# Transposes and division of an attention context moved from TensorE to VectorE, GpSimd and ScalarE

## The reference

```python
x = L0_attn_hidden_states
xn = _layernorm(x, axis=-1)
s = _L0_attn_ref(xn, L0_attn_Wq, L0_attn_Wk, L0_attn_Wv, L0_attn_Wo)
g = _silu(_L0_ffn_ref(xn, L0_ffn_w_gate, L0_ffn_w_up, L0_ffn_w_down))
x = x + s * g
...
```

```python
q = (x @ Wq).reshape(b, t, N_HEADS, HEAD_DIM).transpose(0, 2, 1, 3)
k = (x @ Wk).reshape(b, t, N_KV, HEAD_DIM).transpose(0, 2, 1, 3)
v = (x @ Wv).reshape(b, t, N_KV, HEAD_DIM).transpose(0, 2, 1, 3)
q = _apply_rope(q, cos, sin)
k = _apply_rope(k, cos, sin)
k_h = jnp.repeat(k, GROUP_SIZE, axis=1)
v_h = jnp.repeat(v, GROUP_SIZE, axis=1)
scores = jnp.einsum('bhqd,bhkd->bhqk', q, k_h) / math.sqrt(HEAD_DIM)
causal = jnp.triu(jnp.ones((t, t), dtype=bool), k=1)
scores = jnp.where(causal[None, None], jnp.finfo(scores.dtype).min, scores)
attn = jax.nn.softmax(scores, axis=-1)
ctx = jnp.einsum('bhqk,bhkd->bhqd', attn, v_h)
ctx = ctx.transpose(0, 2, 1, 3).reshape(b, t, D_OUT)
return ctx @ Wo
```

## Time and profile before

| | |
|---|---|
| three executions | 1332.64, 1336.5, 1327.77 us, median 1332.64 |
| the profiled execution | 1332.45 us, its span 1330.7 us |
| mean granted clock of TensorE | 0.98 of full speed |
| busy share of the span | PE 91%, PEld 68%, DVE 61%, ACT 49%, POOL 29% |
| the chain that ended last, by engine | PE 71%, DVE 14%, ACT 8%, issue 4%, DMA 2% |
| instructions | PE 8860, DVE 1322, ACT 1106, POOL 460 |

### The profile page before, as it was taken

One profiled execution on the slowest core, in us unless ns is written; L12 is line 12 of the kernel. 1 busy time (PEld: TensorE's weight loads), 2 busy tenths in 40 slices (PEclk: granted clock), 3 DMA queues, 4 the chain that ended last, 5 costly groups with the idle time before them and its releaser, 6 DMA issues.

```text
span 1330.7 us, 22702 instructions
## 1 busy us (share of the span) xinstructions
PE 1216.5 (91%) x8860; PEld 900.0 (68%) x8860; DVE 808.3 (61%) x1322; ACT 652.6 (49%) x1106; POOL 385.9 (29%) x460
## 2 busy tenths in 40 slices
PE   4999999999999999979999999999899889898897
PEld 3788876666656556546777787776666666676664
DVE  8743467665675645674655566536776776765444
ACT  3333357555454555554333333336665655565653
POOL 1000125333210101021344434405532342424443
PEclk9999989999999999979999999899999999999999
DMA  6000000110000100001242222120001001000001
GB/s 254 0 1 0 1 34 3 48 58 2 1 2 2 36 1 1 26 25 48 72 142 95 95 72 80 64 80 3 2 2 40 2 2 34 1 25 23 2 1 63
DMA packets 15259, 48.07 MB, mean 36 GB/s; under 512 B 2858, under 2 KB 6959, under 8 KB 14388
## 3 DMA queue, kind: packets, MB, share of 16 engines
q1 hardware_dynamic: 15156, 46.63, 10.1%
HBM read 44.00 MB, written 2.10 MB: 35 GB/s over the span
## 4 chain that ended last, share of the span: by engine, by line
PE 71%; DVE 14%; ACT 8%; issue 4%; DMA 2%; POOL 0%; POOLq 0%; DVEq 0%; ACTq 0%; SPq 0%
PE bank L650 18%; PE bank L766 14%; PE bank L680 8%; PE bank L909 8%; PE bank L869 6%; PE bank L817 4%; PE bank L783 3%; DVE negmax L1816 3%; ACT probs L1381 3%; PE bank L849 2%; ACT pv L1389 2%; PE bank L880 2%; DMA W_lo_whole<-in_w 2%; PE bank L797 1%; PE bank L826 1%
## 5 line engine op out<-in xcount | busy, mean ns | idle before, releaser
L1816 DVE TENSOR_REDUCE negmax<-bank 128x4 f32<-128x1024 f32 (+1 forms) x256 | 250.3, 1017 | 77.0 <-PE bank L826 66.2
L1381 ACT ACTIVATE probs<-bank 128x1024 f32<-128x1024 f32 (+1 forms) x256 | 218.0, 865 | 46.0 <-PE bank L849 37.7
L2023 POOL TENSOR_SCALAR_AFFINE_SELECT probs<-probs 128x512 f32<-128x512 f32 x192 | 125.9, 666 | 292.3 <-ACT probs L1381 292.1
L1966 POOL TENSOR_TENSOR W_lo<-W_lo_whole,W_hi 128x1536 fp32r<-128x1536 f32 x28 | 98.4, 3516 | 155.8 <-ACT W_hi L1132 155.8
L817 PE MATMUL bank<-kT,qT 64*128 64x256 f32 (+1 forms) x1024 | 110.5, 312 | 30.1 <-DVE negmaxT L1834 8.8
L817 PEld LDWEIGHTS bank<-kT,qT 64*128 64x128 f32 x1024 | 81.4, 191 | 65.9 <-issue 33.2
L869 PE MATMUL bank<-probs,V 128*32 128x256 f32 (+1 forms) x2048 | 119.6, 352 | 6.6 <-DVE negmax L1816 5.1
L1389 ACT ACTIVATE pv<-bank 128x256 f32<-128x256 f32 x128 | 49.2, 384 | 154.1 <-PE bank L869 153.6
L849 PE MATMUL bank<-qT,kT 64*128 64x256 f32 (+1 forms) x640 | 113.4, 384 | 3.7 <-DVE h_lo_whole L1638 1.6
L1132 ACT ACTIVATE W_hi<-W_lo_whole 128x1536 fp32r<-128x1536 f32 x28 | 41.7, 1488 | 130.6 <-DVE W_lo_whole L1592 130.6
L650 PE MATMUL bank<-xT_hi,W_hi 128*128 128x512 f32 x224 | 91.7, 410 | 5.6 <-ACT silu L1145 4.5
(11 more groups left out here) (205 smaller groups left out, 2692.3 us busy)
## 6 DMA issues: line engine op xcount, KB each, us to landing
W_lo_whole<-in_w SPq DMA_DIRECT2D x28, 768.0 KB, 4.1
Wqkv_lo_whole<-in_Wqkv SPq DMA_DIRECT2D x6, 768.0 KB, 6.7
Wo_lo_whole<-in_Wo SPq DMA_DIRECT2D x4, 1024.0 KB, 4.9
Wqkv<-in_Wqkv SPq DMA_DIRECT2D x2, 1536.0 KB, 7.5
...
```

The lines of the kernel that those rows point to most:

```text
L1381: nc.scalar.activation(A[l].probs[gi % 2][kb][:, :, q0 - kb * A[l].probs1:].rearrange("p (b h) q -> p b h q", b=2), B.tensor(key)[:, :, 0: ...
L1816: v.tensor_reduce(A[l].negmax[u % 2][:, qb, :].rearrange("p (b h) -> p b h", b=2)[:, :, 2 * g:2 * g + 2], B.tensor(key)[:, :, 0:2 * nk].re ...
L1966: gp.tensor_tensor(lo, whole, hi.bitcast(F32), ALU.subtract).then_inc(w_low.sem, 1)
L2023: gp.affine_select(out=blk, in_=blk, compare_op=ALU.is_ge, fill=0.0, base=0, pattern=[[0, 4], [1, P]], channel_multiplier=-1).then_inc(cau ...
```

## The change

The context is no longer turned by TensorE. After `take_pv`, VectorE's `turn_values` transposes `pv` (128x256, in SBUF) in blocks of 32x32 within the tile, which puts each head's sums in a column, and takes their reciprocals (128x8). GpSimd's `scale_context` multiplies the turned block by them (128x8x16), for two groups into one tile `scaled`. VectorE's `turn_context` turns that tile of a pair of groups in blocks of 32 again, in even slots, into one of RING = 6 context tiles of 128x256, whose rows stand as `project_out` needs them. In the layers with split products ScalarE's `context_high` rounds each such tile off and GpSimd's `context_low` takes the difference. `turn_rows`, `take_rows` and VectorE's `context_low` are gone, and so is the bank of turned contexts; `values_bank` is now 6, and 4 near the end of a run. The rows of the output weights are laid out in the new order by the host. `residual` uses the tile of the gate in place of `ctxr`. The split of the last output weights goes by the table `WO3_SLOTS`. In `ffn3` the last projection of outputs stands one chunk later. SP's loads are written as slots, as the other engines' are. In the diff below each engine's edits stand in this order: TensorE, ScalarE, VectorE, GpSimd.

```diff
+RING = 6
+WO3_SLOTS = {(10, 1): (0,), (10, 2): (1, 2), (10, 3): (3,)}
-def values_bank(l, U, g):
-
-    return 7 if not GQA[l] and g % 2 == 0 and U + 1 + g // 2 < RUN else 4
+def values_bank(U, g):
+
+    return 6 if U + 2 + g % 2 < RUN else 4
+def pair_turned(G):
+
+
+    return (G - 4) // 2 if G >= 4 and G % 2 == 0 else None
...
-            def turn_context(r, G, slot, bank=None):
...
-            def turn_rows(l, b, tau, bank):
...
-                pe.wait_ge(*B.emptied(("ctxT", l, b, tau)))
+                pe.wait_ge(*(ctx_low if GQA[l] else ctx_turned).at(l, 4 * (b + 1)))
...
-                if G >= 2:
-                    turn_context(r, G - 2, G)
...
-                for n in rows_turned(r, U, g):
-                    turn_rows(*n, OUT_BANK[n[2]])
...
-                        turn_context(1, last - 1, last)
                         weigh_values(1, last, last)
-                    if e == CHUNKS3_EARLY + 1:
-                        turn_context(1, last, last)
-                        for tau in range(2):
-                            turn_rows(3, SEQS - 1, tau, 6 + tau)
-                    if e == CHUNKS3_EARLY + 2:
+                    if e == CHUNKS3_EARLY + 3:
...
                 act.wait_ge(*B.filled(key))
+                if G >= 2:
+                    act.wait_ge(*values_turned.at(*next_of(r, G - 2)))
                 nc.scalar.activation(A[l].pv[gi % 2][:], B.tensor(key)[:, 0:SEQ], copy).then_inc(B.empties(key), 1)
...
-            def take_rows(l, b, tau):
...
+            def context_high(r, q):
+                l, qi = pair(r, q)
+                if GQA[l]:
+                    act.wait_ge(*ctx_turned.at(l, qi + 1))
+                    nc.scalar.activation(ctx_hi[r][:, q % RING, :], ctx_whole[r][:, q % RING, :], copy).then_inc(ctx_high.sem, 1)
...
                 if G >= 1:
                     take_pv(r, G - 1)
+                if pair_turned(G) is not None:
+                    context_high(r, pair_turned(G))
...
-                context(0, last - 1)
-                context(0, last)
+                turn_values(0, last - 1)
+                turn_context(0, last // 2 - 1)
+                turn_values(0, last)
                 scale_weights(CHUNKS2_EARLY + 1)
                 hidden(2, CHUNKS2_EARLY)
+                turn_context(0, last // 2)
...
-            def context(r, G):
+            def turn_values(r, G):
+
                 l, gi = group(r, G)
...
+                dve.wait_ge(*B.emptied(("PV", l, gi)))
                 if G >= 2:
...
+                    dve.wait_ge(*ctx_scaled.at(*next_of(r, G - 2)))
+                v.transpose(A[l].pvT[gi % 2][:].rearrange("p b r -> p (b r)"), A[l].pv[gi % 2][:]).then_inc(values_turned.sem, 1)
+                dve.wait_ge(*values_turned.at(l, gi + 1))
+                v.reciprocal(A[l].recip[gi % 2][:], A[l].pvT[gi % 2][:, :, HD]).then_inc(rs_ready.sem, 1)
+
+            def turn_context(r, q):
+
+                l, qi = pair(r, q)
+                if q >= RING:
+                    ll, qq = pair(r, q - RING)
+                    dve.wait_ge(*B.filled(("O", ll, qq // 4, 1)))
+                dve.wait_ge(*ctx_scaled.at(l, 2 * qi + 2))
+                v.transpose(ctx_whole[r][:, q % RING, :], A[l].scaled[q % 2][:].rearrange("p b r -> p (b r)")).then_inc(ctx_turned.sem, 1)
...
                 if G >= 2:
-                    context(r, G - 2)
+                    turn_values(r, G - 2)
+                if pair_turned(G) is not None:
+                    turn_context(r, pair_turned(G))
...
+            def scale_context(r, G):
+                l, gi = group(r, G)
+                q = G // 2
+                if q >= 2:
+                    ll, qq = pair(r, q - 2)
+                    pool.wait_ge(*ctx_turned.at(ll, qq + 1))
+                pool.wait_ge(*rs_ready.at(l, gi + 1))
+                gp.tensor_tensor(A[l].scaled[q % 2][:, :, HD * (G % 2):HD * (G % 2 + 1)], A[l].pvT[gi % 2][:, :, 0:HD],
+                                 A[l].recip[gi % 2][:].unsqueeze(2).to_broadcast([P, SEQ // 32, HD]),
+                                 ALU.mult).then_inc(ctx_scaled.sem, 1)
+
+            def context_low(r, q):
+                l, qi = pair(r, q)
+                if GQA[l]:
+                    pool.wait_ge(*ctx_high.at(l, qi + 1))
+                    gp.tensor_tensor(ctx_lo[r][:, q % RING, :], ctx_whole[r][:, q % RING, :],
+                                     ctx_hi[r][:, q % RING, :].bitcast(F32), ALU.subtract).then_inc(ctx_low.sem, 1)
...
                 if CAUSAL[l]:
                     cut_future(r, G)
+                if G >= 2:
+                    scale_context(r, G - 2)
...
+                if pair_turned(G) is not None:
+                    context_low(r, pair_turned(G))
```

More of the change, by code:

```diff
@@ L1765, in ffn3 @@
                     if e == CHUNKS3_EARLY:
[L1766 removed]
+                        turn_values(1, last)
+                        turn_context(1, last // 2 - 1)
                     if e == CHUNKS3_EARLY + 1:
[L1768 to L1771 removed]
+                        turn_context(1, last // 2)
+                    if e == CHUNKS3_EARLY + 3:
                         for tau in range(2):
@@ L2037, in slot @@
                     wqkv_low_part(3, g)
-                if r == 1 and U == 10:
-                    wo_low_part(3, g)
+                if r == 1:
+                    for c in WO3_SLOTS.get((U, g), ()):
+                        wo_low_part(3, c)
                 if r == 1 and (U, g) in SPLIT3_SLOTS:
```

209 lines of the change are left out of this document (95 added, 114 removed).

## The result

The changed kernel took 1300.95 us in the median of four executions (1296.24 to 1305.54). The ratio to the kernel before on the same chip is 0.9765, 95% interval 0.9737 to 0.9793. Measured again later beside other kernels it took 1296.94 us, ratio 0.9734 (0.9708 to 0.9761). I use 0.975 as the mean of the two, some 33 us of gain. The forecast was a gain of 16.6. The profiled execution is the slowest of its four, with a span of 1303.8 us.

The account below looks back on a forecast made before the run. TensorE was taken as the bound on average, gated in places by ScalarE's exponentials and VectorE's maxima. Terms -8.4, -9.1, +3.7 and -2.6 summed to -16.4 us, from 1332.45 to 1316 us; range 1280 to 1348.

Parts of the forecast that it names:

- What leaves TensorE: TensorE's removed matmuls: 128 pairs at 0.31 us and 32 fours at 0.49, a ceiling of 55.4 us.
- Layers 0, 2, 3: Attention slots of the split layers: 0.6 us gained per eight slots, 12 eights, with the last units -8.4 us in sum.
- Layer 1: Its 32 slots, without ScalarE's copy: 24 gain 0.31 us, 6 fours 0.49, two late slots cost 0.6 each; -9.1 us.
- Start of layer 2's feed-forward: Last output projection of layer 1 waits for VectorE's turn behind `hidden`: +2.0 us, +1.7 for the lower clock, +3.7.
- Start of layer 3's feed-forward: Two pairs, two fours and two waits go, 3.5 us, less 0.9 for the new chain over three engines: -2.6 us.
- TensorE bound in every slot: Rival for all slots: ScalarE is early, so all 55.4 us of removed TensorE work arrive, 1277 us; chance 0.16.
- VectorE as the new bound: Rival for first slots of 16 units: VectorE's turn takes 0.69 us, +12, so 1328 us, no change; chance 0.20.
- Exponentials held in all pairs: Rival for 48 slot pairs of split layers: ScalarE's exponentials wait 1.1 us for VectorE's turn, 1351 us; chance 0.14.
- GpSimd holding VectorE: Rival for VectorE's rotations and maxima's followers: GpSimd's 104 us of new work delays VectorE, +8, 1324 us; chance 0.10.

Follow-up runs that it names:

- the kernel with the early turn: The change with VectorE's last turn of layer 1 ahead of the feed-forward's hidden(2, 2) instead of behind it: 1292.4 us, ratio 0.9684 to the kernel before.

## Why the prediction was wrong in size

The direction, the durations and the main waits held, and the times lie in the stated range of 1280 to 1348. But the forecast of 1316 was short by half of the gain, for these steps.

**What leaves TensorE.** A pair was put at 0.31 us and costs 0.21 to 0.23 when put back, a four at 0.49 and costs some 0.43. The ceiling was thus some 42 us and not 55. This made the forecast too large, not too small.

**Layers 0, 2, 3: the step that failed.** I had -0.6 us for eight slots, 12 times. The table above has -2.0 to -2.5, so some -26 us for -7.2. Term by term: slot 1 of even units was to lose 0.7 and loses 0.53 to 0.84. Slot 2 was to gain 0.5 and does. The first of odd units was to gain 0.5, and gains 0.5 to 0.9. Slot 3 was to gain 0.8 and gains only 0.3 to 0.6, an error the other way. The other three slots of odd units were +0.1, -0.1, -0.1 and are -0.07, -0.28, -0.18. And slot 0 of even units gains 0.5 to 0.7, where I had listed nothing. The terms that I wrote down add up to -1.2; I then "made" 0.6 of them, so that this slot stood at a loss of 0.6 without a row. It was the largest single error, 1.2 us an eight, 14 us in all. What the slot gains is in part TensorE's stream and bank: the pair put back costs it 0.23 us, the old bank 0.1 to 0.2, and all together 0.4 of its 0.6; the other 0.2 stays open. The second are the other slots of odd units, -0.5 where I had -0.1, 5 us in all. In slots 1 and 3 I charged ScalarE's copy with 0.45 us, and it costs 0.13 and 0.04 (the run with the copy late); slot 2 has no copy, and there the old bank costs 0.2 to 0.4.

**Not costed at all: the bank.** The text went through every operation and never through `values_bank`. It is worth 6 to 10 us in time and 12.7 in undisturbed slots. It was in the view: L817 waits for `pv` 26 times before, 7.4 us. Part of it lies in the slots of the step above, so the two do not add.

**Layer 1**, forecast -9.1, has -9.8 in undisturbed slots (-8.3 in the second execution). In the profiled execution only -4.9 arrived with 34 us at the lower clock, in that of the second measurement -11.4 with 7; before had 20.

**Start of layer 2's feed-forward.** Forecast +3.7 with a wait of 3.7 us and a stretch at the lower clock. After:

```profile
622.41 3.54 DVE L1598 TENSOR_TENSOR h_lo<-h_lo_whole,h_hi 128x512 fp32r<-128x512 f32 x1 [1.47 <-ACT h_hi L1141]
625.87 0.43 DVE L1832 STREAM_TRANSPOSE ctxT_lo_whole<-scaled 128x256 f32<-128x256 f32 x1
...
626.45 1.19 PE L906 MATMUL bank<-Wo_lo_whole,ctxT_lo_whole 128*128 128x512 f32 x1 [2.63 <-DVE ctxT_lo_whole L1832]
```

The turn stands behind h_lo as said, 2.63 us, and the lower clock ran from 626.05 to 629.46. From the last weighing of run 0 to the first of run 1 the change lost 2.8 us in one execution (10 us at the lower clock, 7 before) and 0.7 in the other (7), less than the 3.7 forecast. **Start of layer 3's feed-forward**: forecast -2.6, but the stretch from the last weighing but one to the end took 65.1 us before and 66.8 and 66.1 after, both with 14 to 16 us of lower clock at the end where before had 1.5. That the clock hid the gain shows in the kernel with the early turn, whose code is the same here: it had 3.1 us of lower clock at the end and took 62.1, which is 3.0 less than before.

**The rivals.** TensorE bound in every slot would have given 1277. In undisturbed slots it is close (pairs at full price in most slots), in the time it is not. VectorE as the new bound fell, as its turn takes 0.43 us. Exponentials held in all pairs fell: ScalarE waited 4.5 us in 48 copies, all of it in eight of them. GpSimd holding VectorE is there but small: the rotation's four operations went from 97.7 us before to 106.7, 9 us more on VectorE, and fell to 99.1 without GpSimd's product; doubling the product cost some 3 us in undisturbed slots and nothing in the time.

**What stays open.** With TensorE's stream and bank as before, 11 us of gain are left. Undisturbed slots give +6 there, slot 1 of even units above all. In the first slots of odd units 1.1 us each went (8.24 to 7.15 in units 5 and 7 of run 1), and in slot 3 of unit 14 of run 0 4.6, where TensorE had waited 3.0 us for ScalarE's row copy, and where before had 3.4 us of lower clock. How the 11 us divide between such waits and the clock I can't say; the price of the lower clock below takes 2 off the 7.5 between the profiled spans (1330.7 and 1323.2).

## What to carry over

List what an edit does to the banks and queues before its operations: here a changed bank was worth more than half of what the removed pairs were. Sum a slot-by-slot forecast as it stands; a correction without a row was the largest error here. And when TensorE is relieved, look whether the engine behind it (here ScalarE, whose exponentials it now awaits for 44 us) lets the gain through.

## What the chip showed beside it

How much time goes at the lower clock differs from execution to execution of one kernel. The same program, at the same wait of 3.12 us in slot 3 of unit 13 of run 0, in the change's first measurement (the timeline row, then the window behind it) and then the same two for its second:

```profile
555.33 0.58 PE L829 MATMUL bank<-kT,qT 64*128 64x256 f32 x2 [3.12 <-DVE negmaxT L1813]
```

```profile
554.40:578.20 23.80, 20.18 (x145) 12.50 (x146) 18.11 (x28) 10.12 (x14) 1.90 (x4) 0.50 0.11 34
```

```profile
549.53 0.80 PE L829 MATMUL bank<-kT,qT 64*128 64x256 f32 x4 [3.12 <-DVE negmaxT L1813]
```

```profile
549.50:573.30 23.80, 16.40 (x163) 10.56 (x164) 20.39 (x33) 14.13 (x19) 4.81 (x6) 0.93 0.13 39
```

At 1.2 GHz 145 matmuls ran in 23.8 us, at a mean of 0.93 163 did. The two executions have 89 and 43 us at the lower clock and spans of 1303.8 and 1287.2, so a microsecond at the lower clock cost 0.36, as their undisturbed slots are alike. Taken off the profiled spans at this price, an estimate from two executions, it leaves these differences to the change: the pairs 21 us slower, the product on VectorE 10, GpSimd's product twice 5, the late copy 5 faster, the early turn the same, and the kernel before 39 slower. That is near the undisturbed slots (18.5, 9, 3, -7, 0 and 34 us). For the pairs, VectorE's product and the early turn it is nearer to them than to the times. Six executions of this kernel ran from 1288.9 us at a clock of 0.984 to 1302.7 at 0.966. So a difference of 5 us between two kernels here may be one of draws unless the undisturbed slots show it too.

GpSimd's product took 1.75 us once, beside VectorE's scaling of weights of 1.71:

```profile
618.62 1.71 DVE L1577 TENSOR_TENSOR W_lo_whole<-W_lo_whole,block_scales 128x1536 f32<-128x1536 f32 x1
618.85 1.75 POOL L1991 TENSOR_TENSOR scaled<-pvT,recip 128x128 f32<-128x128 f32 x1 [3.58 <-DVE recip L1823]
```

The product takes 0.44 us on average and ended 0.27 us behind VectorE's operation. The Trainium skill (SBUF — State Buffer, SBUF: two separate sides) calls this an exclusive lock of a shared port pair between a GpSimd operation and a VectorE one that has two inputs in SBUF or runs in a two-port mode. The trace agrees. A turn, with one input, was not held: 43 of the 128 ran beside a GpSimd operation and took 433 ns, the other 85 took 434, and with GpSimd's product doubled the mean was 433.
